# Graph network kernel: edge batches of 14 tiles with a triangular comparison, and counts of earlier matches moved to ScalarE

## The reference

```
edge_index = stack([src, dst])
x = x + L0_gnn(layernorm(x), edge_index, edge_weight)   # 2 GCN layers, normalised by degree, |weights|
x = x + L0_ffn(layernorm(x))                            # 8 experts, top 2, hidden 1024, per token
x = x + L1_gnn(layernorm(x), edge_index, edge_weight)   # 5 layers: h @ weight[i], sum over edges, GRU cell
x = x + L1_ffn(layernorm(x))                            # 8 experts, top 2 chosen by the mean token
```

## Time and profile before

| | us |
|---|---|
| median of 3 runs | 4075.37 |
| lowest, highest | 4073.07, 4079.72 |
| the profiled execution, its time | 4078.94 |
| the profiled execution, its span | 4077.3 |

### The profile page before, as it was taken

The page is one execution under the profiler, slowest core; times in us unless marked ns, Lnnn a source line. Parts: engine busy times, 40 slices in busy tenths (PEclk is TensorE's granted clock), DMA queues, the critical chain, the costliest instruction groups (busy, mean ns, idle before and its releaser), DMA issues. The chain is left out here.

```text
span 4077.3 us, 54504 instructions
## 1 busy us (share of the span) xinstructions
PE 3112.3 (76%) x17984; PEld 2749.6 (67%) x17985; DVE 2333.4 (57%) x5541; ACT 1249.7 (31%) x2259; POOL 1433.6 (35%) x922
## 2 busy tenths in 40 slices
PE   2545552200799994988858999999999999999698
PEld 2544441100688893877747988998998898899555
DVE  7999992410587886544556455455555455554423
ACT  0000000110344552322324444444444444444132
POOL 1577777767766775777740000000000000000000
PEclk9999996655899996989978999999999999999799
DMA  9655544575667665444245333343333343333100
GB/s 398 214 124 142 123 117 80 124 216 127 163 170 205 165 158 166 100 103 119 37 103 185 124 124 121 125 134 123 124 126 123 121 136 120 125 127 99 47 21 21
DMA packets 381090, 538.34 MB, mean 132 GB/s; under 512 B 126115, under 2 KB 283978, under 8 KB 377482
## 3 DMA queue, kind: packets, MB, share of 16 engines
q1 hardware_dynamic: 251076, 487.82, 35.3%
q0 software_dynamic: 119088, 19.33, 8.4%
q10 hardware_dynamic: 10774, 29.17, 2.0%
HBM read 398.99 MB, written 137.24 MB: 132 GB/s over the span
## 5 line engine op out<-in xcount | busy, mean ns | idle before, releaser
L490 POOL DMA_INDIRECT plane_a<-pair,slot x392 | 652.3, 1664 | 365.9 <-issue 139.5
L598 PE MATMUL bank<-ring_hi,h_hi 128*128 128x448 f32 x1750 | 653.0, 373 | 60.4 <-DVE ring_lo L1624 55.0
L1624 DVE TENSOR_TENSOR ring_lo<-ring_lo,ring_hi 128x448 fp32r<-128x448 f32 x875 | 523.2, 622 | 221.1 <-ACT ring_hi L1075 220.5
L598 PE MATMUL bank<-ring_lo,h_hi 128*128 128x448 f32 x1750 | 644.0, 368 | 0.0
L598 PE MATMUL bank<-ring_hi,h_lo 128*128 128x448 f32 x1750 | 643.7, 368 | 0.0
L1075 ACT ACTIVATE ring_hi<-ring_lo 128x448 fp32r<-128x448 f32 x875 | 497.4, 576 | 385.8 <-PE bank L598 379.6
L546 POOL DMA_DIRECT2D v_lo<-gru_v x5 | 3.6, 722 | 1389.0 <-PE bank L598 1314.1
L598 PE MATMUL bank<-gring_hi,hs_hi 128*128 128x512 f32 (+2 forms) x700 | 261.2, 373 | 294.0 <-DVE gring_lo L1339 294.0
L490 POOL DMA_INDIRECT plane_w<-pair,slot x224 | 384.2, 1715 | 156.0 <-DMA plane_w<-pair,slot 83.1
L598 PEld LDWEIGHTS bank<-ring_hi,h_hi 128*128 128x128 f32 x1750 | 331.3, 189 | 89.5 <-DVE h_lo L1691 48.8
L571 PE MATMUL bank<-parts,eq 128*128 (+1 forms) x3136 | 133.2, 170 | 317.4 <-DVE hit_hi L1287 316.7
(11 more groups left out here) (326 smaller groups left out, 5938.4 us busy)
## 6 DMA issues: line engine op xcount, KB each, us to landing
ring_lo<-plane_w SPq DMA_DIRECT2D x175, 1120.0 KB, 5.4
gring_lo<-plane_a SPq DMA_DIRECT2D x50, 1280.0 KB
plane_a<-nat SPq DMA_DIRECT2D x25, 1600.0 KB, 45.0
plane_w<-nat SPq DMA_DIRECT2D x100, 400.0 KB
w_hl<-w_split SPq DMA_DIRECT2D x16, 2048.0 KB
keyrow<-key_rows ACTq DMA_DIRECT2D x49, 512.0 KB
part_in<-in_L_ffn_W SPq DMA_DIRECT2D x16, 1024.0 KB
w_split<-part_hi SPq DMA_DIRECT2D x16, 1024.0 KB, 4.4
```

The lines of the kernel that those rows point to most:

```text
L490: g_.indirect_dma_start(out=plane, out_offset=bass.IndirectOffsetOnAxis(slot[:, t:t + 1], 0), in_=pair[:, k, t:t + 1], in_offset=None, com ...
L598: last = mm(ps, lhs[x], rhs[y], start=start and n == 0, stop=stop and n == 2)
L1624: V.tensor_tensor(ring_lo[:, t, :], ring_lo[:, t, :].bitcast(FP32), ring_hi[:, t % HS, :].bitcast(FP32), ALU.subtract).then_inc(lo_rdy, 1)
```

## The change

Batches have G = 14 tiles (NB = 28), and there are two key buffers, not four, laid over other tiles of this stage. The comparison is triangular: tile q is tested against the tiles 0 to q of its batch alone, so 105 blocks of 128 x 128 for a batch (`UP`), and TensorE multiplies only these. `before`, `own`, `own_n` and `parts1` are gone. The matches in preceding tiles of the batch are now counted by ScalarE (`count_before`: a copy with an accumulated sum over the first q blocks of row q, for q = 1 to 13). Matches in preceding lanes of the same tile are read from the sums: column 6 of `parts0` holds a power of two that falls with the lane (2^60 for lane 0, 2^-67 for lane 127), and an edge has an earlier match when the sum of its column is more than 2.5 times its own power. VectorE waits for the counts in `compare` and in `place`. The number of scatters of `plane_w` before the experts is W1 = 17 batches of 14, so 238 instead of 224. The wait of the write-backs of the weight parts has new numbers. The loop of the fills of `plane_w` has the same text.

```diff
-G = 8
-KB = 4
+G = 14
+KB = 2
 NB = ET // G
-W1 = 28
-BP, P0 = 30, 4
+UP = G * (G + 1) // 2
+W1 = 17
+BP, P0 = 16, 4
...
+        passed = sb("passed", [EP, 2, (G - 1) * EP], BF16); before_n = sb("before_n", [EP, 2, G])
...
+        eq = sb("eq", [EP, 2, UP * EP], BF16)
+        eq_row = lambda c, q, lo, hi: eq[:, c, (q * (q + 1) // 2 + lo) * EP:(q * (q + 1) // 2 + hi) * EP]
...
+        keyrow = (front[:, 0:G * EP], spare[:, KD * NP - G * EP:KD * NP])
...
-                sp.wait_ge(scat_a, 16 * G * (BP + n))
+                sp.wait_ge(scat_a, 16 * G * (BP + n * 9 // 15))
                 sp.wait_ge(part_l, n + 1)
...
+            g_.iota(order_i[:, :], [[0, 1]], base=187, channel_multiplier=-1).then_inc(consts, 1)
...
                 for g in range(G):
-                    for q in range(G):
-                        parts = (parts1 if q < g else parts0)[:, bass.ds(n * G + q, 1), :].rearrange("p a k -> p (a k)")
-                        mm(ps_sum[c][:, g, :], eq[:, c, q, g * EP:(g + 1) * EP], parts, start=(q == 0), stop=(q == G - 1))
+                    parts = lambda q, cols: parts0[:, bass.ds(n * G + q, 1), 0:cols].rearrange("p a k -> p (a k)")
+                    mm(ps_sum[c][:, g, :], eq_row(c, g, g, g + 1), parts(g, 8), start=True, stop=(g == G - 1))
+                    for q in range(g + 1, G):
+                        mm(ps_sum[c][:, g, 0:6], eq_row(c, q, g, g + 1), parts(q, 6), start=False, stop=(q == G - 1))
...
+            def count_before(n, c):
+                act.wait_ge(compared, n + 1 + KB)
+                act.wait_ge(placed, n + 1)
+                for q in range(1, G):
+                    act.wait_ge(passed_on, n * (G - 1) + q)
+                    A(passed[:, q % 2, 0:q * EP], eq_row(c, q, 0, q), ACT.Copy, accum_out=before_n[:, c, q:q + 1]).then_inc(passed_on, 1)
+                act.wait_ge(passed_on, (n + 1) * (G - 1) + 2)
+                act.sem_inc(counts, 1)
+
             def take_sums(n, c):
+                count_before(n, c)
                 act.wait_ge(summed, n + 3)
...
+            link(V.tensor_scalar(order[:, :].bitcast(I32), order_i[:, :], 23, None, ALU.logical_shift_left))
+            go(V.tensor_copy(parts0[:, :, 6], order[:, :].to_broadcast([EP, ET])))
+            go(V.tensor_scalar(beyond[:, :], order[:, :], 2.5, None, ALU.mult))
...
-                for g in range(G):
-                    V.tensor_scalar(eq[:, c, g, :], keyrow[:, b, :], at(key, g), None, ALU.is_equal)
-                for g in range(G):
-                    V.scalar_tensor_tensor(own[:, c, g, :], keyrow[:, b, g * EP:(g + 1) * EP], at(key, g), before[:, :], ALU.is_equal, ALU.mult, accum_out=own_n[:, c, g:g + 1])
+                v.wait_ge(counts, n + 1)
+                for q in range(G):
+                    V.tensor_scalar(eq_row(c, q, 0, q + 1), keyrow[b][:, 0:(q + 1) * EP], at(key, q), None, ALU.is_equal)
...
             def place(n, c):
                 v.wait_ge(sums_out, n + 3)
+                v.wait_ge(counts, n + 3)
...
-                link(V.tensor_tensor(earlier[:, c, :], sums[:, c, :, 6], own_n[:, c, :], ALU.add))
+                link(V.scalar_tensor_tensor(earlier[:, c, :], sums[:, c, :, 6], beyond[:, 0:1], before_n[:, c, :], ALU.is_gt, ALU.add))
```

More of the change, by code:

```diff
@@ L162, in build @@
         lo_i, hi_i, spare_i = (early[:, m, :].bitcast(I32) for m in (5, 6, 7))
-        srci = sb("srci", [EP, ET], I32); dsti = sb("dsti", [EP, ET], I32); w = sb("w", [EP, ET])
+        w = sb("w", [EP, ET])
         wabs = sb("wabs", [EP, ET]); key = sb("key", [EP, ET])
[L165 to L168, removed]
+        dlo, dhi = srcf, dstf
+        to_spare = sb("to_spare", [EP, ET])
+        parts0 = sb("parts0", [EP, ET, 8], BF16)
+        order_i = sb("order_i", [EP, 1], I32); order = sb("order", [EP, 1]); beyond = sb("beyond", [EP, 1])
         hit_lo = sb("hit_lo", [EP, 2, G, 128]); hit_hi = sb("hit_hi", [EP, 2, G, NT])
-        own = sb("own", [EP, 2, G, EP], BF16); own_n = sb("own_n", [EP, 2, G])
+        passed = sb("passed", [EP, 2, (G - 1) * EP], BF16); before_n = sb("before_n", [EP, 2, G])
         sums = sb("sums", [EP, 2, G, 8]); half = sb("half", [EP, 2, G, 2])
@@ L180, in build @@
         spare = xT[:, :, :].rearrange("p k n -> p (k n)")
+        keyrow = (front[:, 0:G * EP], spare[:, KD * NP - G * EP:KD * NP])
+        keyT = eq[0:ET // 4, 0, 0:8 * EP].bitcast(FP32).rearrange("t (c p) -> t c p", c=4)
+        srci, dsti = (eq[:, 1, 2 * ET * n:2 * ET * (n + 1)].bitcast(I32) for n in range(2))
         wt_sb = spare[:, 0:LAYERS * KD * D].rearrange("p (i k f) -> p i k f", i=LAYERS, k=KD)
@@ L258, in build @@
         keyrow_in = [sem(f"keyrow_in{b}") for b in range(KB)]
-        compared = sem("compared"); summed = sem("summed"); sums_out = sem("sums_out"); placed = sem("placed")
+        compared = sem("compared"); counts = sem("counts"); passed_on = sem("passed_on"); summed = sem("summed"); sums_out = sem("sums_out"); placed = sem("placed")
         scat_a = sem("scat_a"); scat_w = sem("scat_w"); deg_done = sem("deg_done")
@@ L466, in _ @@
             g_ = nc.gpsimd
-            g_.memset(srci[:, :], NP - 1).then_inc(padded, 1)
-            g_.memset(dsti[:, :], NP).then_inc(padded, 1)
+            g_.memset(srci, NP - 1).then_inc(padded, 1)
+            g_.memset(dsti, NP).then_inc(padded, 1)
             g_.memset(w[:, :], 0.0).then_inc(padded, 1)
@@ L473, in _ @@
             g_.memset(ident[:, :], 0.0).then_inc(consts, 1)
-            g_.memset(before[:, :], 1.0).then_inc(consts, 1)
+            g_.iota(order_i[:, :], [[0, 1]], base=187, channel_multiplier=-1).then_inc(consts, 1)
             g_.memset(below[:, :], 1.0).then_inc(consts, 1)
@@ L481, in _ @@
             g_.affine_select(out=ident[:, :], in_=ident[:, :], compare_op=ALU.not_equal, fill=1.0, base=0, pattern=[[-1, 128]], channel_multiplier=1).then_inc(consts, 1)
-            g_.affine_select(out=before[:, :], in_=before[:, :], compare_op=ALU.is_gt, fill=0.0, base=0, pattern=[[-1, EP]], channel_multiplier=1).then_inc(consts, 1)
             g_.affine_select(out=below[:, :], in_=below[:, :], compare_op=ALU.is_gt, fill=0.0, base=0, pattern=[[1, 128]], channel_multiplier=-1).then_inc(consts, 1)
@@ L558, in _ @@
             mm(ps_deg, zeros[:, 0:128], zeros[:, 0:NT], start=True, stop=False)
-            pe.wait_ge(consts, 10)
+            pe.wait_ge(consts, 9)
             pe.wait_ge(key_done, 1)
@@ L892, in _ @@
             act.sem_inc(sums_out, 2)
+            act.sem_inc(counts, 2)
+            act.sem_inc(passed_on, 2)
             act.wait_ge(keyT_ps, 1)
@@ L917, in _ @@
             for n in range(KB * LOOPED, NB):
-                if n + KB < NB:
-                    load_keys(n + KB, (n + KB) % KB)
                 take_sums(n, n % 2)
@@ L1248, in _ @@
             v.wait_ge(edges_in, 16 * 9)
-            go(V.tensor_copy(srcf, srci[:, :]))
-            link(V.tensor_copy(dstf, dsti[:, :]))
+            go(V.tensor_copy(srcf, srci))
+            link(V.tensor_copy(dstf, dsti))
             V.scalar_tensor_tensor(key[:, :], srcf, float(NP), dstf, ALU.mult, ALU.add).then_inc(key_done, 1)
-            go(V.tensor_scalar(lo_i, dsti[:, :], 127, None, ALU.bitwise_and))
-            go(V.tensor_scalar(hi_i, dsti[:, :], 7, None, ALU.logical_shift_right))
+            go(V.tensor_scalar(lo_i, dsti, 127, None, ALU.bitwise_and))
+            go(V.tensor_scalar(hi_i, dsti, 7, None, ALU.logical_shift_right))
             go(V.tensor_scalar(wbits.bitcast(I32), w[:, :].bitcast(I32), 0x7fffffff, None, ALU.bitwise_and))
             go(V.memset(wabs[:, :], 1e-6))
-            go(V.memset(parts0[:, :, :], 0.0))
-            link(V.memset(parts1[:, :, :], 1.0))
+            go(V.memset(before_n[:, :, 0:1], 0.0))
+            link(V.memset(parts0[:, :, :], 0.0))
+            v.wait_ge(key_done, 1)
             go(V.tensor_copy(dlo[:, :], lo_i))
@@ L1260, in _ @@
             go(V.tensor_scalar(finite, wbits, FLT_MAX, None, ALU.is_le))
-            v.wait_ge(consts, 10)
+            v.wait_ge(consts, 9)
+            link(V.tensor_scalar(order[:, :].bitcast(I32), order_i[:, :], 23, None, ALU.logical_shift_left))
+            go(V.tensor_copy(parts0[:, :, 6], order[:, :].to_broadcast([EP, ET])))
+            go(V.tensor_scalar(beyond[:, :], order[:, :], 2.5, None, ALU.mult))
             link(V.tensor_copy(to_spare[:, :], spare_i))
@@ L1300, in _ @@
             compare(0, 0, 0)
-            with ch.loop(0, NB // KB, 2 * KB) as i:
+            LOOPED = NB // KB - 1
+            with ch.loop(0, LOOPED, 2 * KB) as i:
                 for b in range(KB):
@@ L1304, in _ @@
                     place(KB * i + b, b % 2)
-            place(NB - 1, (NB - 1) % 2)
+            for n in range(KB * LOOPED, NB):
+                if n + 1 < NB:
+                    compare(n + 1, (n + 1) % KB, (n + 1) // KB)
+                place(n, n % 2)
             def rest_of_part(n):
```

6 lines of the change are left out of this document (1 added, 5 removed).

## The result

The changed kernel takes 4196.53 us (median of 4 runs, 4194.42 to 4204.5), the kernel before in the same comparison 4077.55. The ratio is 1.0297, with a 95% interval of 1.0279 to 1.0314: slower by 119 us. The forecast was 4193 with a range of 4145 to 4240. The profiled execution took 4195.84 us, its span is 4194.2, 116.9 more than before.

What follows compares the result with a forecast made beforehand. GpSimd's scatters bound the front, then TensorE's GCN, then GpSimd in the experts; with SyncE's fills now deciding, GCN 154 us later minus 36 in the experts gave +118 on 4078.94, 4197, so 4193 against the median; range 4145 to 4240.

Steps and rivals of the forecast that it cites:

- Last fill: SyncE's last zeroing DMA of the second plane, waiting for 350 of 392 scatters: 126 + 430 + 316 = 872 us.
- The second rival: GpSimd scatters slowed by longer compares, 2.43 us with issue: last fill 943, 71 later, kernel 4264 us; chance 0.08.
- VectorE's end: VectorE's batches of comparison and placing start at 50 us and end near 50 + 28 x 18 = 554 us.
- ScalarE's count: 13 counting copies a batch on ScalarE: 9.9 + 2.2 + 2.4 = 14.5 us, hidden, costing nothing up to 29 us a batch.
- From the last fill to the ring loads: SyncE's chain of part loads, write-backs and GCN weights: from last fill at 872 to ring loads from 1190 us.
- Last scatter into the GCN plane: GpSimd's first-plane scatters over at 872 + 3 x 29 = 959 us, no longer deciding the GCN's start.
- Experts: Expert stage paced by GpSimd, 154 late scatters and 11 drains: shortens by 0 to 40 us, 36 taken.
- Chance of "faster": Rival that scatters still end last: ring loads at 960, 76 us earlier, kernel 3963 us; chance 0.04.

Runs made afterwards that it cites:

- experiments 1 and 2: 1: changed kernel, fills of the second plane paced as before the change, 4026.56 us; 2: kernel before, only those fills paced by 14, 4262.55 us.
- mixing: Each comparison followed by two hit tests, not 14 comparisons in one run: on the changed kernel 4217.18 us, with fills also paced as before 4036.81 us.
- Experiment 1: Changed kernel with the fills of the second plane paced as before, last group waiting for 210 scatters instead of 350: 4026.56 us, ratio 0.9875.

## Why the prediction was right, step by step

The mechanism held, and experiments 1 and 2 show it from both sides: with the fills by 8 the change is 52 us faster than before, and with the fills by 14 the old kernel is 184 slower.

- *Last fill*: 872, measured 890.6. The term that was off is the scatter with VectorE busy: taken from before at 1.68, measured 1.83, 160 of them, so 24 us too few; the first scatter began 2 later too, and VectorE's earlier end gave some back. Batches were 30.9 to 37.9 us apart while VectorE compared, not 29 to 31. The second rival named the longer scatters and priced one at 2.13; its case came true by a third. The Trainium skill (SBUF — State Buffer, SBUF: two separate sides) has the two engines shut each other out for one whole instruction. The holds of 5.83 and 5.85 us went beyond that: the first lasted 4.3 us of its run of comparisons, and the widest one takes 1.14. Nothing I read from the rule foretold that, nor that mixing would make the mean worse.
- *VectorE's end*: 554, measured 506. Its batches start 16.0 us apart on the mean (28 of them, from 45.7 to 478.2) and not 18. My own terms add to 19.5, and I went on with 18. Both are too high, since I added the busy times of the two hit tests, which overlap: the two of a tile start 0.4 us after those of the last tile, not 0.59. The clean way is the distance from batch to batch. It cost nothing, since VectorE then waits 394 us.
- *ScalarE's count*: 14.5 us, measured 12.2 from the first copy of a batch to the last accumulator (61.05 to 73.28 us). The groups by line:

```profile
L916 ACT ACTIVATION_READ_ACCUMULATOR passed<-eq 128x1 f32 x364 | 68.0, 187 | 0.0
...
L916 ACT ACTIVATE passed<-eq 128x1664 bf16<-128x1664 bf16 x28 | 44.1, 1574 | 0.0
```

  1574 ns for 1664 columns is the 0.85 ns a column and 0.17 fixed of the forecast (1.58), and the means of the 13 copies add to 12.15. The term that was off is the reading of the accumulator, 2.4: it overlaps the copies on both sides by some 0.1 us, and costs next to nothing. The 13.6 us that I had estimated from the Trainium skill (ScalarE: Activation LUTs, Rules for kernel authors) lie between 12.2 and 14.5.
- *From the last fill to the ring loads*: 318, measured 301. The first write-back came after 12.5 us instead of 18 (the 8 us that I gave to the fills ahead of the load were too many), and a part took (1180.15 - 1017.05)/11 = 14.8 instead of 15.4. VectorE's block was 69.2 instead of 72. These 17 us cancel the 19 of the first point by luck: the 1190 for the ring loads (1191.86) is closer than its terms deserve.
- *Last scatter into the GCN plane*: 959, measured 988. Three batches follow the last fill, and I gave them 29 us each. Their starts, with the one ahead of them:

```profile
859.57 1.55 POOL L492 DMA_INDIRECT plane_a<-pair,slot  x1 [2.13 <-DMA plane_a<-pair,slot]
...
888.80 1.55 POOL L492 DMA_INDIRECT plane_a<-pair,slot  x1 [2.19 <-DMA plane_a<-pair,slot]
...
929.52 1.55 POOL L492 DMA_INDIRECT plane_a<-pair,slot  x1 [6.30 <-DMA plane_a<-pair,slot]
...
963.66 1.55 POOL L492 DMA_INDIRECT plane_a<-pair,slot  x1 [7.04 <-DMA plane_a<-pair,slot]
```

  The one ahead took 29.2 us, the next two 40.7 and 34.1, with the weight parts beginning at 890.60. It cost nothing, since the ring loads wait for SyncE's list. Whether the traffic of the parts or the work of VectorE and ScalarE on them holds the scatters, no run tells apart.
- *Experts*: 36 less, measured 41.1. I kept back 4 for weight loads, which did not show. The step without GpSimd is 7.05, not 6.70.
- *Chance of "faster"*: the figure for the scatters ending last, 76 us earlier ring loads, was far too good even where SyncE's list did not bind. Experiment 1 got 13.4: its 28 batches took 32 us each, not 29.8. The figure missed the longer scatters beside comparisons, and that batches beside the weight parts take longer.

## What to carry to other kernels

When a batch size changes, look for every wait that counts in batches, also in loops that the diff does not show: here a pacing wait on another queue moved from 51% to 89% of the scatters, and what stood behind it became the critical path. Work taken off an engine is worth what waits for that engine; ask first which queue issues the next stage. And where an engine must wait for its own DMAs to land, independent DMAs to another target fill the wait.

## What the hardware showed that I had not expected

- Indirect accumulating DMAs that all land in a small area (1792 words of 4 bytes, in one run) were slow to land: drains took 224.8/26 = 8.6 us, up to 13.8, against 68.5/27 = 2.5 when they are spread over the plane.
- The length of a GpSimd scatter's issue depends on which operations VectorE runs, not only on how busy it is: 1.55 to 1.58 us with VectorE idle or in its other work of this stage, 1.76 to 1.82 beside the comparisons of batches of 8, 2.02 to 2.18 beside the triangular ones.
- Some scatters are held up to the end of a whole run of comparisons: 5.83 us in the changed kernel and up to 7.27 with the wide comparisons in two. Each of the 13 scatters over 2.5 us of that run, from 130 to 500 us, ended 0.2 or 1.5 us behind the end of a run of comparisons.
- Reading ScalarE's accumulator after a copy (187 ns each, 13 a batch) costs next to nothing: 13 copies with their reads take 12.23 us, and the copies alone add to 12.15.
